# Second half group in its own PSUM bank, picks on GpSimd's queue, one shifted half by GpSimd: a window and grid attention block with an S4D layer

## Time and profile before

| | us |
|---|---|
| median of 3 runs (lowest, highest) | 220.65 (220.43, 223.14) |
| the profiled execution: its time | 219.83 |
| its span from the first to the last instruction | 218.0 |
| busy in it: TensorE, DVE, ACT, GpSimd | 195.2, 148.1, 127.4, 101.4 |
| mean granted clock of TensorE | 0.977 of 2.4 GHz |

### The profile page before, as it was taken

The page is one execution under the profiler, slowest core; times in us unless marked ns, Lnnn a source line. Parts: engine busy times, 40 slices in busy tenths (PEclk is TensorE's granted clock), DMA queues, the critical chain, the costliest instruction groups (busy, mean ns, idle before and its releaser), DMA issues.

```text
span 218.0 us, 6353 instructions
## 1 busy us (share of the span) xinstructions
PE 195.2 (90%) x2559; PEld 101.3 (46%) x2559; DVE 148.1 (68%) x302; ACT 127.4 (58%) x248; POOL 101.4 (46%) x221
## 2 busy tenths in 40 slices
PE   7659979797988789898979997899999999999992
PEld 2125444445544344434344443445555566666581
DVE  0877467756682686738969798982332668988883
ACT  2363676776655647666556709855546666565560
POOL 8367435455772131776797032410000356775551
PEclk9995899999999999999999999999999999999996
DMA  6932900000000000030000000370000000000000
GB/s 179 216 55 65 222 9 5 3 3 0 6 0 3 0 3 0 3 99 6 3 5 0 0 3 5 77 158 15 0 0 0 0 3 3 14 11 11 14 11 21
DMA packets 3810, 6.70 MB, mean 31 GB/s; under 512 B 1606, under 2 KB 2774, under 8 KB 3686
## 3 DMA queue, kind: packets, MB, share of 16 engines
q1 hardware_dynamic: 2485, 3.68, 7.6%
q0 software_dynamic: 624, 1.71, 3.2%
q10 hardware_dynamic: 672, 0.92, 1.7%
HBM read 4.53 MB, written 0.40 MB: 23 GB/s over the span
## 4 chain that ended last, share of the span: by engine, by line
PE 59%; DVE 14%; ACT 9%; issue 6%; SPq 4%; POOL 3%; DMA 3%; POOLq 0%; DVEq 0%; ACTq 0%
PE ps L1917 13%; PE ps L1952 13%; PE ps L1707 3%; PE ps L1793 3%; PE ps L1751 3%; PE ps L1685 3%; DVE x L1303 2%; DMA bias<-tab_b 2%; SPq L441 2%; PE ps L1763 2%; PE ps L1697 2%; PE ps L1653 2%; PE ps L1728 2%; PE ps L1667 2%; DVE ks L1196 2%
## 5 line engine op out<-in xcount | busy, mean ns | idle before, releaser
L1793 PE MATMUL ps<-fill 128*128 128x512 f16 x110 | 31.7, 415 | 1.4 <-DVE fill L1378 1.2
L1243 DVE TENSOR_REDUCE mx<-ps 128x16 f32<-128x784 f32 (+3 forms) x18 | 15.9, 890 | 16.7 <-PE ps L1667 16.6
L879 ACT CAST q_hi<-ps 128x392 f16<-128x392 f32 (+1 forms) x30 | 13.8, 511 | 12.0 <-PE ps L1617 11.6
L906 ACT ACTIVATE pr<-ps 128x784 f32<-128x784 f32 (+3 forms) x18 | 13.7, 759 | 12.1 <-PE ps L1707 12.0
L786 POOL TENSOR_TENSOR pr<-pr 128x448 f16<-128x448 f32 x7 | 7.4, 1063 | 27.1 <-ACT pr L1085 27.1
L1793 PEld LDWEIGHTS ps<-fill 128*128 128x128 f16 x110 | 10.3, 105 | 13.9 <-issue 4.3
L1061 ACT ACTIVATE pt<-ps,ybias 128x448 f32<-128x448 f32 x14 | 8.9, 634 | 12.9 <-PE ps L1917 12.0
L1952 PE MATMUL ps<-vm_buf,wglu_hi 128*128 128x448 f16 x56 | 15.1, 352 | 0.0
L1303 DVE STREAM_TRANSPOSE x<-u 96x448 f32<-96x448 f32 (+4 forms) x12 | 13.9, 1155 | 1.8 <-ACT u L959 1.5
L1917 PE MATMUL ps<-u4hi,gw_hi 128*128 128x448 f16 x56 | 12.9, 353 | 2.1 <-ACT u4hi L1043 1.5
L1085 ACT CAST pr<-pr 128x448 f16<-128x448 f32 x14 | 7.9, 564 | 10.1 <-DVE pr L1544 10.1
(11 more groups left out here) (277 smaller groups left out, 518.9 us busy)
## 6 DMA issues: line engine op xcount, KB each, us to landing
xr<-x SPq DMA_DIRECT2D x3, 392.0 KB, 5.5
wglu<-w_glu POOLq DMA_DIRECT2D x1, 512.0 KB, 4.5
out<-u SPq DMA_DIRECT2D x7, 56.0 KB, 1.6
x<-x_win SPq DMA_DIRECT2D x2, 168.0 KB, 4.8
u4hi<-ust_s SPq DMA_DIRECT2D x4, 84.0 KB, 2.5
par_g<-stage_g POOLq DMA_DIRECT2D x1, 274.5 KB
x<-x_win ACTq DMA_DIRECT2D x2, 112.0 KB, 5.8
x<-x_win POOLq DMA_DIRECT2D x2, 112.0 KB, 5.1
```

Source lines behind the costliest of these rows:

```text
L879: nc.scalar.copy(q_hi[:, i % 4, 0:cw], qk_bank(k, i)[:, 0:cw]).then_inc(s_qkhi[k], 1)
L906: nc.scalar.activation(dst[:, :, 0:cw], ps[:, 2:4, 0:cw], ACT.Exp).then_inc(s_exp[k], 1)
L1243: nc.vector.tensor_reduce(m[:, :, 0:n], ps[:, bank:bank + 2, 0:n * T].rearrange("p h (j m) -> p h j m", m=T), AX.X, ALU.max).then_inc(s_mx ...
L1793: nc.tensor.matmul(ps[:, bank, :], fill[:, 0:128], fill[:, :], start=True, stop=True)
```

## The change

- The picks are loaded first on GpSimd's queue and no longer by SP. Two of the seven bias table transfers go to ACT's queue behind its part of x's first piece. That piece is two chunks instead of three, and the second is three instead of two. SP loads two row blocks of the second piece behind the tables; GpSimd loads none of it and splits the bias before `window_f32(1)`.
- The second half group of `attend` uses bank 2 and follows the first half directly, on TensorE, ACT and DVE. `turned_scores` of the next group, which overwrites bank 2, waits for the second half's `attention_out`. Where three fillers stood around the second half, they stand behind the q/k tiles, and in the last group of stage g there are none. Two of the head's fillers are gone.
- The shift 3 of the first chunk's `u4hi` is written by GpSimd instead of DVE.

```diff
-PIECES = ((0, 3), (3, 5), (5, 7))
+BIAS_BY_SP = 5
+PIECES = ((0, 2), (2, 5), (5, 7))
...
+        def attend_bank(half):
+            return ps[:, 2 if half else 6, :]
...
-            sp.dma_start(sel[:, :], pick).then_inc(s_sel, 16)
...
                 if k == "g":
+                    image_piece(1)
                     image_piece(2)
...
-                for y in range(s):
+                for y in range(BIAS_BY_SP if k == "b" else s):
...
+            pool.dma_start(sel[:, :], pick).then_inc(s_sel, 16)
             pool.dma_start(par["b"][0:96, 0:288], stage_b[0:96, 0:288]).then_inc(s_pb, 16)
...
-            first, last = PIECES[1]
-            for i in range(2):
-                pool.dma_start(x1[32 * i:32 * i + 32, first * CW:last * CW],
-                               x_win[:, first * CW:last * CW]).then_inc(s_xp, 16)
             pool.wait_ge(s_x[0], 48)
...
+            split_bias("b")
             window_f32(1)
-            split_bias("b")
...
+            pool.wait_ge(s_gnr, 6)
+            nc.gpsimd.tensor_scalar(u4hi[96:128, PAD + 3:PAD + 3 + CW], x1[64:96, 0:CW], gr[64:96, 1, 0:1],
+                                    gr[64:96, 1, 1:2], ALU.mult, ALU.add).then_inc(s_firstlop, 1)
...
             image_piece(0)
+            for y in range(BIAS_BY_SP, 7):
+                act.dma_start(bias32[y * 7:(y + 1) * 7, :, 0:49],
+                              tab_b[:, :, (6 - y) * 7:(6 - y) * 7 + 49]).then_inc(s_tab["b"], 16)
             nc.scalar.preload_act_table_set("natural_log_exp_and_others")
...
+                if u:
+                    act.wait_ge(s_rec[k], u)
+                nc.scalar.activation(den[:, 0:w], attend_bank(half)[:, 256:256 + w], ACT.Ln).then_inc(s_ln[k], 1)
...
                     row_inverse(k, g, 0)
+                    if len(halves_of(k, g)) > 1:
+                        row_inverse(k, g, 1)
                     if k == "b" and g == 0:
                         window_f32(3)
...
-                    if len(halves_of(k, g)) > 1:
-                        row_inverse(k, g, 1)
...
                         spread_max(k, g + 1)
+                    if len(halves_of(k, g)) > 1:
+                        attention_out(k, g, 1)
                     for i in (8 + 4 * g, 9 + 4 * g):
                         if i < 2 * n:
                             qk_split(k, i)
-                    if len(halves_of(k, g)) > 1:
-                        attention_out(k, g, 1)
...
-            for s in range(2, 4):
-                ins = nc.vector.tensor_scalar(u4hi[32 * s:32 * s + 32, PAD + s:PAD + s + CW], x1[64:96, 0:CW],
-                                              gr[64:96, 1, 0:1], gr[64:96, 1, 1:2], ALU.mult, ALU.add)
+            nc.vector.tensor_scalar(u4hi[64:96, PAD + 2:PAD + 2 + CW], x1[64:96, 0:CW], gr[64:96, 1, 0:1],
+                                    gr[64:96, 1, 1:2], ALU.mult, ALU.add).then_inc(s_firstd, 1)
...
                 if u:
                     pe.wait_ge(s_exp[k], u)
+                    if hp == 0 and len(halves_of(k, g - 1)) > 1:
+                        pe.wait_ge(s_on[k], halves_done(k, g - 1))
...
-                if u:
+                bank = attend_bank(half)
+                if half == 0 and u:
                     pe.wait_ge(s_on[k], u)
-                else:
+                elif u == 0:
                     pe.wait_ge(s_qks[k], 7)
...
-            keep_running(11)
+            keep_running(10)
...
-            keep_running(5)
+            keep_running(4)
...
                     attend(k, g, 0)
+                    if len(halves_of(k, g)) > 1:
+                        attend(k, g, 1)
                     for i in (8 + 4 * g, 9 + 4 * g):
                         if i < 2 * n:
                             qk(k, i)
...
-                    dense = k == "b" and g in (1, 2)
-                    if not dense:
-                        keep_running(1)
-                    if len(halves_of(k, g)) > 1:
-                        attend(k, g, 1)
-                    if not dense:
-                        keep_running(2)
+                    if not (k == "b" and g in (1, 2) or k == "g" and g == last):
+                        keep_running(3)
...
             pe.wait_ge(s_firstd, 1)
+            pe.wait_ge(s_firstlop, 1)
```

More of the change, by code:

```diff
@@ L189, in vit_s4d_kernel @@
         s_cst, s_pb, s_pg, s_par, s_wg = (sem(n) for n in ("consts_in", "par_b_in", "par_g_in", "s4d_in", "wglu_in"))
-        s_xp = sem("x_piece1_rows_by_pool")
         s_x = [sem(f"x_piece{i}_in") for i in range(len(PIECES))]
@@ L451, in _ @@
                     sp.wait_ge(s_firstd, 1)
+                    sp.wait_ge(s_firstlop, 1)
                 for s in range(4):
@@ L458, in _ @@
                     sp.wait_ge(s_firstlo, 1)
-                    sp.wait_ge(s_firstlop, 1)
+                    sp.wait_ge(s_firstlop, 2)
                 for s in range(2, 4):
@@ L685, in window_f32 @@
                 pool.wait_ge(s_gnr, 3)
-                pool.wait_ge(s_x[n], 16)
-                pool.wait_ge(s_xp, 32)
+                pool.wait_ge(s_x[n], 48)
                 step(nc.gpsimd.tensor_scalar(u32[32:64, c], x1[32:64, c], gr[32:64, 0, 0:1], gr[32:64, 0, 1:2],
@@ L768, in _ @@
             pool.wait_ge(s_gws, 2)
+            pool.wait_ge(s_gnr, 6)
+            nc.gpsimd.tensor_scalar(u4hi[96:128, PAD + 3:PAD + 3 + CW], x1[64:96, 0:CW], gr[64:96, 1, 0:1],
+                                    gr[64:96, 1, 1:2], ALU.mult, ALU.add).then_inc(s_firstlop, 1)
+            pool.wait_ge(s_firstlop, 1)
             pool.wait_ge(s_u32, 2)
@@ L772, in _ @@
                                     ust["s"][64:96, 0:CW], ALU.subtract).then_inc(s_firstlop, 1)
-            pool.wait_ge(s_firstlop, 1)
+            pool.wait_ge(s_firstlop, 2)
             for seg, (first, last) in enumerate(SEGMENTS):
@@ L860, in window_hi @@
                 c = slice(n * 784, (n + 1) * 784)
-                act.wait_ge(s_x[(0, 1, 2, 2)[n]], 16 if n == 1 else 48)
-                if n == 1:
-                    act.wait_ge(s_xp, 32)
+                act.wait_ge(s_x[(0, 1, 2, 2)[n]], 48)
                 for c in ((slice(0, 392), slice(392, 784)) if n == 0 else (c,)):
@@ L918, in row_inverse @@
                     act.wait_ge(s_on["b"], halves_done("b", groups["b"] - 1))
-                nc.scalar.activation(den[:, 0:w], ps[:, 6, 256:256 + w], ACT.Ln).then_inc(s_ln[k], 1)
+                if u:
+                    act.wait_ge(s_rec[k], u)
+                nc.scalar.activation(den[:, 0:w], attend_bank(half)[:, 256:256 + w], ACT.Ln).then_inc(s_ln[k], 1)
                 act.wait_ge(s_ln[k], u + 1)
@@ L1272, in attention_out @@
                     dve.wait_ge(s_pj["b"], groups["b"])
-                nc.vector.tensor_tensor(on[:, g % 2, first * T:last * T], ps[:, 6, 0:w], rec[:, u % 2, 0:w],
+                nc.vector.tensor_tensor(on[:, g % 2, first * T:last * T], attend_bank(half)[:, 0:w], rec[:, u % 2, 0:w],
                                         ALU.mult).then_inc(s_on[k], 1)
@@ L1460, in _ @@
             dve.wait_ge(s_padz, 1)
-            for s in range(2, 4):
-                ins = nc.vector.tensor_scalar(u4hi[32 * s:32 * s + 32, PAD + s:PAD + s + CW], x1[64:96, 0:CW],
-                                              gr[64:96, 1, 0:1], gr[64:96, 1, 1:2], ALU.mult, ALU.add)
-            ins.then_inc(s_firstd, 1)
+            nc.vector.tensor_scalar(u4hi[64:96, PAD + 2:PAD + 2 + CW], x1[64:96, 0:CW], gr[64:96, 1, 0:1],
+                                    gr[64:96, 1, 1:2], ALU.mult, ALU.add).then_inc(s_firstd, 1)
             nc.vector.tensor_scalar(u32[:, 0:CW], x1[:, 0:CW], gr[:, 1, 0:1], gr[:, 1, 1:2], ALU.mult,
@@ L1727, in attend @@
                 for h in range(HEADS):
-                    nc.tensor.matmul(ps[32 * h:32 * h + 32, 6, 256:256 + w], weights, p[:, h, first * T:last * T],
+                    nc.tensor.matmul(bank[32 * h:32 * h + 32, 256:256 + w], weights, p[:, h, first * T:last * T],
                                      start=True, stop=True)
@@ L1732, in attend @@
                     for h in range(HEADS):
-                        ins = nc.tensor.matmul(ps[32 * h:32 * h + 32, 6, at:at + T], vm[:, g % 2, j, h, :],
+                        ins = nc.tensor.matmul(bank[32 * h:32 * h + 32, at:at + T], vm[:, g % 2, j, h, :],
                                                p[:, h, j * T:(j + 1) * T], start=True, stop=True)
@@ L1931, in _ @@
                     pe.wait_ge(s_firstlo, 1)
-                    pe.wait_ge(s_firstlop, 1)
+                    pe.wait_ge(s_firstlop, 2)
                 if n in segment:
```

## The result

Over 20 runs of each the changed kernel takes 224.66 us (222.03 to 230.57) and the kernel before 220.01 (218.49 to 224.48). The ratio is 1.0139, 95% interval 1.0105 to 1.0173, slower by 3.1 us, where I had said 217.3. All ratios here are formed from the runs within 1.5% of the fastest of their kernel (11 of 20 of the changed one, 17 of 20 before), while medians are of all runs; so the medians differ by more, 4.7 us. The profiled execution of the changed kernel was timed at 222.92, with a span of 221.1 us and a mean granted clock of 0.956 (before: 219.83, 218.0, 0.977).

A forecast was written before the change was run, and what follows sets the result against it. It took a load, the bias tables, to bound the head, with TensorE nearly always busy from the convolution on. Terms -2.0, -1.95 and +0.7 summed to -3.2, giving 217.3 us, range 215.7 to 220.2.

The forecast's parts named there:

- Attention groups: Block and grid stage groups: running the second half right behind the first costs +0.7 us in sum, bounds 0 and +2.0.
- so that is hidden: Head: two tables on ACT's queue delay table preload, constants and x pieces by 1.6 us, at no cost.
- the term of -2.0: Head: bias tables land at 11.0 instead of 13.03, first score at 14.6; -2.0 us, bounds -0.46 and -2.75.
- -1.95: Head: less idle time keeps the clock from being lowered, so work from tile 4 on shortens; -1.95 us, bounds 0 and -2.4.
- rival (b): Head: tables land when the DMA engines finish x, whichever queue issued them; only -0.46, total 220.9 us; chance 0.09.
- rival (a): Head: the clock falls all the same, leaving -2.0 + 0.7, total 219.4 us; chance 0.25.
- block groups 0 and 1 +0.9, +0.35: Block stage: ACT's second row inverse and DVE's second attention_out delay the q/k splits TensorE awaits; +0.9 and +0.35 us.
- grid group 0 +0.36: Grid stage, group 0: second attention_out goes ahead of the split TensorE waits for; +0.36 us.
- grid groups 2 and 3 -0.43, -0.45: Feed forward held only by GpSimd's halves, -0.43 us; projection starts when attention_out ends, three fillers gone, -0.45 us.
- Rival (c): Groups: q/k tiles pay +1.6 us for the second half, gains of grid groups 2 and 3 vanish; 221.8 us, chance 0.06.
- The new wait: Groups: turned scores waiting for the previous half's attention_out in bank 2; 0, bounds 0 and +0.4 in each of two groups.
- the shifted half at 0: Before the convolution: half moved to GpSimd, DVE saves half a microsecond but still waits for ACT; 0, bounds 0 and +0.3.

The follow-up runs named there:

- the constants first: Kernel before with only the change's head part, both constant loads ahead of the two tables on ACT's queue: median 216.03 us, ratio 0.9861.
- the head by itself: Kernel before with only the change's head part (picks on GpSimd, x first, two tables on ACT's queue, two fillers less): median 217.01 us, ratio 0.9877.
- the groups by themselves: Kernel before with only the groups' part (bank 2, halves back to back on all engines, fillers moved), old head: median 228.86 us, no ratio formed.
- the q/k tiles first: Changed kernel, but ACT and DVE drain the second half behind the q/k tiles in block groups 0, 1 and grid group 0: median 218.79 us, ratio 0.9883.
- the groups' part with fillers: Kernel before with only the groups' part, plus fillers in its six pauses (8, 8, 6; 5, 3, 3): median 222.02 us, ratio 1.0121.
- the remedies together: Changed kernel with constants ahead of tables, q/k tiles drained first and 4, 6, 2 fillers in three groups, shifted half on DVE: median 217.80 us, ratio 0.9936.
- the shifted half by itself: Kernel before with only the shifted half moved to GpSimd: median 220.09 us, ratio 1.0023.
- the changed one with fillers in two pauses: Changed kernel with eight more fillers ahead of the waiting q/k tile in block groups 0 and 1: median 219.81 us, ratio 0.9995.
- the fastest version: Changed head, constants ahead of tables, GpSimd's shifted half; bank 2 and back-to-back halves in grid group 2 only, no fillers in grid group 3: 214.98 us, ratio 0.9811.

## Why the prediction was wrong

Two steps failed. The larger is "Attention groups": its sum adds up waits and has no term for the clock, which cost 4.2 us. The other is the cover under "Head", "so that is hidden": the term of -2.0 came out as +0.5.

**Head, -2.0 and -1.95 forecast, -2.25 measured together.** "On ACT the two delay the table preload, the constants and x pieces by 1.6 us; ACT computes nothing before the statistics, so that is hidden" looked for who computes on ACT, not for who waits for what ACT loads. The constants are wanted by DVE's first split and TensorE's first position matmuls; they were issued 2.7 us later and ended last. I had costed x's second piece and the tables behind their new neighbours, and named this load only among those that are hidden. The tables themselves beat my landing time (by 9.18, forecast 11.0), the opposite of rival (b). Of the gain 2.1 us is the earlier issue (the last at 5.95 instead of 8.05), and the rest is a shorter way from issue to landing, 3.2 us instead of 4.98, which I had left at 5.0. The Trainium skill ("DMA: Bandwidth & Descriptors", Issuing engines are not separate DMA queues) says that transfers of all issuing engines share the same DMA engines, and by it I had put them at 12.6 us. That figure failed, but the page's rule is not refuted by it: the change also put much of x and the constants behind the tables, so less lay ahead of them, and no run separates the two. Since TensorE's pause stayed at 2.33 us the clock fell as in rival (a), but from 14.0 to 17.4 us instead of 16.7 to 23.5. The first score is 0.5 later and all of the head's gain is clock, by luck: I had forecast a clock that does not fall at all, and it fell earlier and for half the time. In the profile with the constants first both terms come out, 4.3 us together.

**Groups, +0.7 forecast.** The sizes of the order's terms were right, forecast and measured in the changed trace: block groups 0 and 1 +0.9, +0.35 and +0.94, +0.27; grid group 0 +0.36 and +0.26; grid groups 2 and 3 -0.43, -0.45 and -0.34, -0.40. Together +0.73 measured. What is missing is a term that the sum does not have: I had asked of the clock only in the head, where it was already low. In the groups I added up who waits for whom and forecast a pause of about 1 us before tile 10; it was 1.97, since the pause between the halves went into it, and I did not ask what the chip grants around it. My own upper bound of +2.0 held no clock either. The clock cost 4.2 us in the profiled execution (with fillers 3.9 of it was back in the profile, 3.2 by the ratios, 4.9 by the medians). Rival (c) had the sign, the places (block groups 0 and 1, grid group 0) and the mechanism of its first half, but not the price: it had +1.6 for them.

**The new wait and the shifted half at 0.** Both as forecast: no wait of TensorE for bank 2 shows in the changed trace, and the shifted half is 1.0023 (0.9972 to 1.0073). The 0 of the wait holds only with `attention_out` moved up in the same change.

**The sum.** Head -2.3, order +0.7, clock +4.2 gives +2.7, the measured shift at the start of the convolution; the last 0.4 of the span lies behind it, where the change touched nothing. My base, the median of three runs, was also 0.6 us above the median of twenty.

## What to carry to other kernels

Where short waits of TensorE are merged into one by running work back to back, price the clock behind the longer pause before the order itself: here 1.2 us of order became 5.4. Reorder only in the groups where the moved work ends last, and leave the others as they are; that, with the constants first, made +1.4% into -1.9%. When a transfer goes into a queue, list every load behind it and who reads each first, on whatever engine.

## What the runs showed that I had not expected

**Pauses and the clock.** Each pause of TensorE of 1.77 to 2.44 us that ended later than 13 us had a low clock beside it, which began within 2.4 us of its end, once 0.8 us before it (15.24 before, 13.46, 30.75 and 44.12 after, 13.58 in the head by itself, 33.41 and 49.39 in the groups by themselves, 26.91 with the q/k tiles first); so had the stop of 3.24 us that ended at 31.31 in the groups' part with fillers. Earlier in the head it is not so regular: of four pauses of 1.78 to 3.28 us that ended at 7.5 to 8.7 us, one (2.56, ended at 8.61 with the groups' part and fillers) had none. Shorter ones went both ways: the wait for GpSimd in block group 2, 1.68 or 1.69 us, stands in six profiles and cost clock in one (49.74 with the remedies together); 1.25 at 51.63 before cost nothing, 1.26 at 89.71 did in another kernel, and 0.49 was the longest ahead of the low clock in the shifted half by itself. The low clock lasted from 3.4 to 14 us. So longer pauses made it more frequent here and did not alone decide it; what does was not settled.

**A bank can move the bottleneck.** That the bank and its wait, with no order changed, make the kernel slower (1.0129) was not in my list.

**Stops without a visible cause.** In eight of the profiles TensorE stops once for 1.1 to 3.2 us within 26 to 32 us, in the middle of a stream of value matmuls that wait for nothing, and the profile says "issue", as here with the constants first:

```profile
28.18 0.41 PE L1734 MATMUL ps<-pr,vm_buf 128*32 128x49 f32 x17 [1.55 <-issue]
```

The kernels before and after, the changed one with fillers in two pauses, the head by itself and the fastest version show none. With the load `xr` moved from 18.7 to 42.7 us there was no such stop at 26 to 32, and one of 1.36 us at 51.80. In all nine profiles with a stop it ended 8.9 to 9.6 us behind the first issue of `xr`, which lay between 17.3 and 22.0 us in the eight and at 42.7 in this one; so it goes with the load and not with a place in the program. By what way the load would hold TensorE, and why five profiles show no stop, stays open.
